# A decoder layer on one core: the biases of the values folded into the output projection, and the values' copies moved from VectorE to ScalarE

## The reference

```python
v = _heads(x @ Wv + bv)
y = jnp.einsum('bhqk,bhkd->bhqd', jax.nn.softmax(att, axis=-1), v)
vc = _heads(cross_input @ Wcv + bcv)
y = y + jnp.einsum('bhqk,bhkd->bhqd', jax.nn.softmax(attc, axis=-1), vc)
return y @ Wp + bp
```

## Time and profile before

| | |
|---|---|
| timed runs, median (lowest, highest) | 2312.41 us (2309.06, 2316.03) |
| span of the profiled execution | 2303.2 us |
| profiled execution's own time beside its span | not recorded; the median of the timed runs lies 9.2 us above the span |
| mean granted TensorE clock | 0.970 |
| PE busy | 2183.0 us (95%) |
| DVE busy | 1869.5 us (81%) |
| ACT busy | 1384.6 us (60%) |
| POOL busy | 189.0 us (8%) |

### The profile page before, as it was taken

One profiled execution on the slowest core, in us unless ns is written; L12 is line 12 of the kernel. 1 busy time (PEld: TensorE's weight loads), 2 busy tenths in 40 slices (PEclk: granted clock), 3 DMA queues, 4 the chain that ended last, 5 costly groups with the idle time before them and its releaser, 6 DMA issues.

```text
span 2303.2 us, 37677 instructions
## 1 busy us (share of the span) xinstructions
PE 2183.0 (95%) x13138; PEld 991.3 (43%) x13138; DVE 1869.5 (81%) x5137; ACT 1384.6 (60%) x2977; POOL 189.0 (8%) x349
## 2 busy tenths in 40 slices
PE   5999999999999999999999999999999999989992
PEld 2354434543345434554335543454334543345432
DVE  6858879788888879788797887978888787978854
ACT  2834687456854579446783467745686457844560
POOL 3011001100011000110001100010001100001000
PEclk7899999999999999999999999999999999999995
DMA  3600034000520006100160002500043000510000
GB/s 110 130 10 1 1 67 81 10 1 1 113 44 10 1 19 121 27 1 1 38 119 10 2 1 58 100 10 1 1 91 57 10 1 11 105 33 1 1 10 9
DMA packets 250845, 81.69 MB, mean 35 GB/s; under 512 B 236064, under 2 KB 247328, under 8 KB 250656
## 3 DMA queue, kind: packets, MB, share of 16 engines
q1 hardware_dynamic: 250656, 79.29, 16.8%
HBM read 16.35 MB, written 4.19 MB: 9 GB/s over the span
## 4 chain that ended last, share of the span: by engine, by line
PE 79%; DVE 10%; ACT 7%; issue 3%; DMA 0%; SPq 0%; POOL 0%; DVEq 0%; POOLq 0%; ACTq 0%
PE bank L1517 23%; PE bank L1570 13%; PE bank L1555 7%; PE bank L1204 7%; PE bank L1513 5%; ACT work L603 4%; PE bank L1552 4%; PE bank L1470 4%; DVE work L770 4%; PE bank L1333 3%; PE bank L1320 2%; PE bank L1356 2%; PE bank L1530 2%; PE bank L1582 1%; ACT k_c L636 1%
## 5 line engine op out<-in xcount | busy, mean ns | idle before, releaser
L659 ACT ACTIVATE work<-bank 128x512 f32<-128x512 f32 (+3 forms) x1536 | 739.7, 550 | 529.8 <-PE bank L1552 264.1
L1033 DVE TENSOR_REDUCE top_half<-bank 128x1 f32<-128x512 f32 x1024 | 625.5, 682 | 21.0 <-PE bank L1517 21.0
L1517 PE MATMUL bank<-k_c,q_c 32*128 32x512 f32 x2048 | 628.6, 634 | 0.0
L1555 PE MATMUL bank<-q_c,k_c 32*128 32x512 f32 x2048 | 526.2, 633 | 0.0
L603 ACT ACTIVATE work<-work,neg 128x512 bf16<-128x512 bf16 x512 | 362.6, 715 | 30.5 <-DVE work L770 29.8
L1517 PEld LDWEIGHTS bank<-k_c,q_c 32*128 32x128 f32 x2048 | 274.6, 184 | 245.1 <-DVE top_half L1033 159.8
L770 DVE TENSOR_SCALAR_CACHE_REDUCE work<-bank 128x512 bf16<-128x512 f32 x512 | 322.4, 686 | 43.7 <-PE bank L1302 33.6
L1570 PE MATMUL bank<-work,v_flat 128*32 128x512 f32 (+3 forms) x3072 | 321.8, 544 | 5.5 <-ACT work L659 5.0
L1030 DVE CUSTOM_DVE_ANT_0 masked<-bank,mask_w 128x384 bf16<-128x384 f32 (+3 forms) x512 | 223.8, 488 | 79.5 <-PE bank L1513 74.0
L1552 PE MATMUL bank<-q_s,k_s 32*128 32x512 f32 (+3 forms) x1024 | 258.1, 471 | 0.0
L1555 PEld LDWEIGHTS bank<-q_c,k_c 32*128 32x128 f32 x2048 | 218.4, 183 | 78.4 <-ACT work L659 48.6
(11 more groups left out here) (194 smaller groups left out, 2214.1 us busy)
## 6 DMA issues: line engine op xcount, KB each, us to landing
xT_pad<-xT SPq DMA_DIRECT2D x16, 256.0 KB, 3.3
ctx_sb<-ctxT SPq DMA_DIRECT2D x8, 512.0 KB, 3.4
x_res<-x SPq DMA_DIRECT2D x8, 512.0 KB, 4.8
out<-r_sb SPq DMA_DIRECT2D x8, 512.0 KB, 3.1
work<-work SPq DMA_TRANSPOSE x112, 4.4
qk_sb<-qkT SPq DMA_DIRECT2D x1, 512.0 KB, 4.7
pe_sb<-pe_w SPq DMA_DIRECT2D x1, 256.0 KB, 4.0
v_sb<-vT SPq DMA_DIRECT2D x1, 256.0 KB, 5.4
```

Of the source, the lines that this page charges most:

```text
L659: nc.scalar.activation(pT[:, s % PT_SLOTS, g, q0:S], exp_bank(n)[:, 0:S - q0], ACT.Exp, scale=SCALE).then_inc(pT_ready, 1)
L1033: nc.vector.tensor_reduce(top_half[:, i % 2, g, u // 2, u % 2:u % 2 + 1], scores, AX.X, ALU.max, negate=True).then_inc(slot_out, 1)
L1517: mm(dst, q_c[rows, i, P * t:P * (t + 1)], k_c[rows, i, S * half:S * (half + 1)], start=True, stop=True, tile_position=(GW * g, 0)).then_i ...
L1555: mm(dst, k_c[rows, i, P * u:P * (u + 1)], q_c[rows, i, :], start=True, stop=True, tile_position=(GW * g, 0)).then_inc(sT_mm, 1)
```

## The change

The two bias rows are no longer kept broadcast over 128 partitions. They arrive as columns (`bv_col`, `bcv_col`), are added, spread to a 128-column tile each (`bv_wide`) and multiplied with the output weights on PE once at setup; the product is added to `bp_row`. The setup chain has 32 links instead of 29. `values(i)` goes from DVE's list to ACT's: for i = 0 to 3 from behind DVE's work of heads 7, 9, 11 and 13 to ACT's list behind the exponentials of heads 8, 10, 12 and 14; for i = 4 behind the third `unit` and ahead of the Gelu; for i = 5 behind the sixth `unit` and ahead of the exponentials. It is a plain copy.

```diff
-        bv_row, bcv_row, bp_row = sb("bv_row", [P, D]), sb("bcv_row", [P, D]), sb("bp_row", [P, D])
+        bv_col, bcv_col, bp_row = sb("bv_col", [P, KD]), sb("bcv_col", [P, KD]), sb("bp_row", [P, D])
+        bv_wide = sb("bv_wide", [P, KD, P])
...
-                   (bv_row[:], bv.partition_broadcast(P)), (bcv_row[:], bcv.partition_broadcast(P)),
+                   (bv_col[:], bv), (bcv_col[:], bcv),
...
+                def values(i):
+
+                    act.wait_ge(vj_mm, FIRST + b * PAIRS + i + 1)
+                    t, at = (NT + 2 * i, 7) if i < CTX_PAIRS else (2 * (i - CTX_PAIRS), VALUES_BANK)
+                    nc.scalar.copy(v_all[:, t:t + 2, :, 0:HD],
+                                   bank[:, at, :].rearrange("p (t h j) -> p t h j", t=2, h=H)).then_inc(vj_evac, 1)
...
+                    if h in (8, 10, 12, 14):
+                        values((h - 8) // 2)
                     if 0 <= h - 8 < 2 * CTX_UNITS:
                         context_key(h - 8)
...
                 units(2)
+                values(CTX_PAIRS)
                 if prev:
                     gelu(c)
                 if prev:
                     compress(c)
                 units(3, 4, 5)
+                values(CTX_PAIRS + 1)
                 for s in range(ALL_STEPS):
                     probabilities(s)
...
-                def values(i):
-
-                    dve.wait_ge(vj_mm, FIRST + b * PAIRS + i + 1)
-                    row, t = (bcv_row, NT + 2 * i) if i < CTX_PAIRS else (bv_row, 2 * (i - CTX_PAIRS))
-                    at = 7 if i < CTX_PAIRS else VALUES_BANK
-                    nc.vector.tensor_tensor(v_all[:, t:t + 2, :, 0:HD], bank[:, at, :].rearrange("p (t h j) -> p t h j", t=2, h=H),
-                                            row[:].rearrange("p (h j) -> p h j", h=H).unsqueeze(1).broadcast_to([P, 2, H, HD]),
-                                            ALU.add).then_inc(vj_evac, 1)
...
-                    if h in (7, 9, 11, 13):
-                        values((h - 7) // 2)
...
-                    if m in VALUES_LEAD:
-                        values(CTX_PAIRS + VALUES_LEAD.index(m))
...
+            link(nc.vector.tensor_tensor(bv_col[:], bv_col[:], bcv_col[:], ALU.add))
+            link(nc.vector.tensor_copy(bv_wide[:], bv_col[:].unsqueeze(2).broadcast_to([P, KD, P])))
+            BIAS_WIDE = setup[0]
             dve.wait_ge(sig_tr, 1)
...
+            link(nc.vector.tensor_tensor(bp_row[:], bank[:, 1, 0:D], bp_row[:], ALU.add))
...
-            pe.wait_ge(sig_ready, 5)
+            pe.wait_ge(sig_ready, 7)
+            project(bank[:, 1, 0:D], lambda k: bv_wide[:, k, :], lambda k: wp_sb[:, k, :])
             for k in range(KD):
                 last = nc.tensor.transpose(bank[:, 0, TILES * k:TILES * (k + 1)], sig_work[:, 0, P * k:P * (k + 1)],
...
+    for n in ("bv", "bcv"):
+        arrays[n] = arrays[n].reshape(2, 128).T
```

More of the change, by code:

```diff
@@ L112, in decoder_layer @@
     FFN_STEPS = 70
-    SIG_STEPS = 29
+    SIG_STEPS = 32
     ctx = ExitStack()
@@ L1182, in _ @@
             link(nc.vector.tensor_scalar(temp[:, 2:3], temp[:, 2:3], -1.0, None, ALU.mult))
-            assert setup[0] == SIG_STEPS and SIG_NAT == 5
+            assert setup[0] == SIG_STEPS and SIG_NAT == 5 and BIAS_WIDE == 7
             convolve(1)
```

## The result

| us | before | after |
|---|---|---|
| timed runs on one chip, median (lowest, highest) | 2311.55 (2309.06, 2316.03) | 2342.48 (2339.02, 2347.14) |
| ratio after to before | | 1.014, 95% interval 1.0119 to 1.0161 |
| span of the profiled execution | 2303.2 | 2337.2 |
| its own time | not recorded | 2339.96 |
| mean granted TensorE clock | 0.970 | 0.963 |

The forecast of 2334 us (2318 to 2350) holds: slower, and within the range. But the sum of its terms was 21.6 us, and the two medians lie 30.9 us apart, the two spans 34.0. The sum was 9 us too small by the medians and 12 by the spans. The measured 2342.48 lies just above the forecast's own range of 2326 to 2341, beside the 2344 of the rival in which the clock falls more often.

What follows compares the result with a forecast made beforehand. ACT was taken to bound the late head loop, PE the run-up. Terms 8.3 + 10.9 + 0 + 2.4 = 21.6 us raise the span 2303.2 to 2324.8, plus 9.2 to 2334.0 us; range 2318 to 2350, own range 2326 to 2341.

Steps and rivals of the forecast that it cites:

- the rival in which the clock falls more often: Around the Gelu, PE's new pause lowers its clock in more batches: 5 to 15 us more, about 10, 2344 us; chance 27%.
- What bounds the kernel: ACT ends last in the head loop's second half, PE leads the run-up; DVE's 33.0 us of removed copies count nothing.
- Head loop, 8.3: ACT's four added copies: pairs 2 and 3 cost 0.94 us in batches 0 to 6, last batch 1.7; 8.3 us.
- The detail that the reciprocals wait from head 9 on: Sign of being right: DVE's reciprocals in the head loop wait for ACT from head 9, by 0.5 to 1 us each.
- The Gelu's pause, 10.9: Batches 1 to 7: pair 4's copy delays the Gelu, PE's product starts 1.9 us late, 0.35 returns; 10.9 us.
- Pair 5, 0: End of run-up: ACT's copy and the table load behind it just fit before the first exponential; 0, at most 1.6 us.
- The rival of a hidden part of the load: Behind a copy, the table load costs some 1.4 us more at the Gelu and delays the exponentials; 2353 us, chance 5%.
- Setup, 2.4: Three added chain links take 1.1 us and PE's projection 1.3 us, delaying the head loop; 2.4 us (2.0 to 3.0).
- The distance from span to own time, 9.2: Median of timed runs lies 9.2 us above the profiled span; the same distance was added to the predicted span 2324.8.

Runs made afterwards that it cites:

- kernel 1: Changed kernel with ACT's copy of pair 4 moved behind the Gelu instead of ahead of it; 2319.41 us, ratio 1.005 to the kernel before.
- kernel 2: Changed kernel with pairs 0 to 3 copied by DVE again, without a bias, pairs 4 and 5 still on ACT; 2328.14 us, ratio 1.0101.
- kernel 3: Changed kernel with all six pairs copied by DVE at their old places, only the folding of the biases left; 2310.86 us, ratio 1.0017.
- kernel 4: Changed kernel with eight spare matmuls on PE in the pause ahead of the Gelu's product; 2318.95 us, ratio 1.0056.
- kernel 5: Changed kernel with pairs 0 and 1 copied by ACT, pairs 2 to 5 by DVE; one run, 2303.09 us.
- kernel 6: Changed kernel with pairs 2 and 3 copied by ACT, the others by DVE; one run, 2314.63 us.
- kernel 7: Changed kernel with pairs 2 and 3 on DVE, 0 and 1 on ACT, pair 4 on ACT behind the Gelu, pair 5 on ACT; 2310.49 us, ratio 1.0015.
- kernel 11: Changed kernel with four spare matmuls in the pause ahead of the Gelu's product, half of kernel 4's eight; one run, 2326.74 us.
- kernel 9: Kernel 5 timed again in five rounds (pairs 0 and 1 on ACT, the rest on DVE); 2308.74 us, ratio 1.0001.

## Why the prediction was right, and where its size was off

**What bounds the kernel: right.** ACT ends last at the end of the head loop, PE in the run-up. DVE's lost 33 us gave nothing: from the first reciprocal to that of head 8, batch 3 was 0.6 us quicker after (33.75 us against 34.35), and ACT's waits took that back by head 15.

**Head loop, 8.3: measured 8.2.** The copy takes 0.586 us and moves the next exponential or context key by 0.47 to 0.48; two of four fit the gap of 0.93. The last batch lost 1.45, not 1.7. Some 0.6 us of the 8.2 is low clock, so the agreement to 0.1 is partly luck. The detail that the reciprocals wait from head 9 on by 0.5 to 1 us each was wrong: in batches 0 to 6 they wait at heads 11 to 14, by 0.80, 0.30, 0.91 and 0.30 us, and only in the last batch from head 9.

**The Gelu's pause, 10.9: the term for the pause right, measured 11.3.** L1289 waited 1.94 us (forecast 1.9), 0.41 came back (0.35).

**Pair 5, 0: right.** Batch 3 after, ACT's timeline at the end of the run-up, beside the earlier trace rows:

```profile
995.67 0.59 ACT L656 COPY v_flat<-bank 128x512 f32<-128x512 f32 x1 [2.60 <-PE bank L1207]
996.27 1.28 ACT L667 ACT_TABLE_LOAD   x1
```

The load follows 0.02 us behind the copy, and the first exponential starts at 997.57, 1.90 us after the copy's start; before, it was 1.92 (974.51 to 976.43). The rival of a hidden part of the load falls with it. The Trainium skill's page "ScalarE: Activation LUTs", section "What ACT_TABLE_LOAD costs", has a drain beside the load's 1.28 us; no run here shows one, behind a copy or behind an activation.

**Setup, 2.4: measured 2.26, in part by luck.** The parts were off in both directions: the spreading copy took 0.29 us (0.42 in the forecast), the projection 2.04 at granted clock 0.50 (1.3 in the forecast), the two additions 0.24 and 0.42. They add up to 2.99 us, but the chain began 0.36 us earlier than before's and its six additions (L1167) took 1.29 us in place of 1.73. With the same setup, the traces of kernels 1 to 7 have the first reciprocal at 52.32 to 54.61 us, before had 51.86; so a single trace gives this term only to about 1 us.

```profile
34.55 0.24 DVE L1159 TENSOR_TENSOR bv_col<-bv_col,bcv_col 128x2 f32<-128x2 f32 x1
34.82 0.29 DVE L1160 COPY bv_wide<-bv_col 128x256 f32<-128x256 f32 x1
35.26 2.04 PE L1207 MATMUL bank<-wp_sb,bv_wide 128*128 128x256 f32 x4 [5.13 <-DVE bv_wide L1160]
...
39.69 0.42 DVE L1168 TENSOR_TENSOR bp_row<-bank,bp_row 128x256 f32<-128x256 f32 x1
```

**The clock: the step that failed.** The sum held nothing for it. It stood as a rival, with 27%, at about 10 us (5 to 15). That rival came true on top of the forecast's own terms, and its size was good: the timed runs miss the sum by 9.3 us, and taking the pause away gave back 8 to 9.5 us of clock in timed runs (kernels 1 to 3). Between the two traces it is 14.6 us in batches 1 to 7. The argument against it ("the pause is short, and in batch 3 the clock held at 1.00 over the same work") looked at a run-up without a pause; it said nothing of one with a pause. The windows of batches 4 and 6 had already shown that the clock falls in this stretch without any pause. That was the row to weigh: a new pause in a stretch that already loses its clock now and then. The Trainium skill's page "TensorE: Matmul & The Clock Gate", Part 1, section "HAM oscillation — how this bites in real kernels", describes waits of PE on transfers, longer than the one here, that are each followed by work at half clock. In this case's trace the wait of 1.94 us was followed by it in six batches of seven, and kernels 4 and 11 show that it is the idleness in the wait that matters.

**The distance from span to own time, 9.2: a wrong reading that cost nothing.** After's profiled execution has 2.8 us, and all other runs of these kernels have 1.7 to 3.0. Before's profiled execution must then have taken about 2306 us, a quick one among its runs (median 2311.55). The forecast is untouched by it: 2303.2 plus 9.2 is the median of before's first three timed runs, so 2334.0 is that median plus the 21.6 us of the terms, and medians are what was compared. But it is why the spans lie 34.0 us apart and the medians 30.9: before's trace was a quicker run, for its kernel, than after's.

**Open.** Why the clock also falls without a pause wasn't settled: two tails of seven in before and kernel 3, five in kernel 1, all seven in kernel 6 (the seventh by only 0.3 us), and one and three in the two traces of kernels 5 and 9, which are the same program. Shown is that the clock falls less where the pause is filled (kernels 4 and 11) or gone (kernel 1).

## What to carry to other kernels

Before moving an instruction to a less busy engine, ask what stands behind it there: a copy of 0.59 us, put ahead of a table load and a Gelu that had run hidden, became a pause of 1.94 us on the bounding engine, because ACT takes its list in order and the copy had to wait for PE first. Price a new pause of PE twice, once for its length and once for the clock behind it; here the second was nearly as large as the first (8 to 9.5 us beside 11.3 in timed runs, 14.6 between the two traces). And take an idle gap as room only once: in batches 0 to 6 the same copy was free in the two places of the head loop where ACT had 0.93 us, and cost its full 0.47 us in the next two.

## What the runs showed of the hardware

- A pause of 1.94 us on PE was followed by work at 1.2 GHz in six of seven batches. Eight spare matmuls in it (1.90 us) kept 2.4 GHz in seven of seven, four in three of seven. Without any pause there the clock fell too, in two of seven before and five of seven in kernel 1, so filling won more (19.5 us in the tails) than the pause had cost the clock (8 to 14 us).
- A fall of the clock cost 1.7, 3.0 or 6.9 us in a batch (tails of 22.28, 23.67 and 27.52 us against 20.63), so a pause of one fixed length has no fixed price.
- Twelve runs of one kernel spread by 17 us (2299.70 to 2316.70, median 2308.74); a single run can't tell a change of under 0.4% here.
